# Attention in a two-layer kernel: four banks for the scores, probabilities turned back into the bank of their scores, two turnings in a row

## The reference, cut to what matters

```
NUM_HEADS = 16; NUM_GROUPS = 4; KEY_WIDTH = 64
Q = (X @ Wq).reshape(n, s, NUM_GROUPS, HEADS_PER_GROUP, KEY_WIDTH)
K = (X @ Wk).reshape(n, s, NUM_GROUPS, KEY_WIDTH)
V = (X @ Wv).reshape(n, s, NUM_GROUPS, VALUE_WIDTH)
raw = jnp.einsum('bsgwe,btge->bstgw', Q, K * scale)
attn = jax.nn.softmax(raw, axis=2)
A = jnp.einsum('bstgw,btge->bsgwe', attn, V).reshape(n, s, NUM_HEADS * VALUE_WIDTH)
P = A @ Wpost
return X + P
```

## Time and profile before

| what | us |
|---|---|
| median of 3 runs | 2735.33 |
| fastest and slowest of them | 2728.69, 2736.3 |
| the profiled execution | 2734.21 |
| its span, first to last instruction | 2732.1 |

### The profile page before, as it was taken

One profiled execution on the slowest core, in us unless ns is written; L12 is line 12 of the kernel. 1 busy time (PEld: TensorE's weight loads), 2 busy tenths in 40 slices (PEclk: granted clock), 3 DMA queues, 4 the chain that ended last, 5 costly groups with the idle time before them and its releaser, 6 DMA issues.

```text
span 2732.1 us, 38184 instructions
## 1 busy us (share of the span) xinstructions
PE 2280.7 (83%) x13155; PEld 1424.3 (52%) x13192; DVE 1884.1 (69%) x2830; ACT 1796.4 (66%) x3310; POOL 1738.2 (64%) x1416
## 2 busy tenths in 40 slices
PE   5776769999688889898989898989898988987781
PEld 4444547776445446554645465546544644554451
DVE  5779835553246786687668856876677667788788
ACT  3556834445367776788578857785787677765763
POOL 1000054434766998688878878877987797655565
PEclk9888989999899989899999999999999999998895
DMA  4000158874555667555755475447553854476786
GB/s 157 24 20 5 37 143 242 245 221 101 95 112 113 131 138 168 114 114 117 174 105 114 99 177 115 101 93 181 109 104 82 190 107 89 93 173 146 166 185 144
DMA packets 281904, 344.46 MB, mean 126 GB/s; under 512 B 66031, under 2 KB 211390, under 8 KB 281712
## 3 DMA queue, kind: packets, MB, share of 16 engines
q0 software_dynamic: 84080, 175.67, 34.4%
q1 hardware_dynamic: 175120, 144.80, 18.4%
q10 hardware_dynamic: 22512, 21.57, 2.3%
HBM read 198.23 MB, written 26.80 MB: 82 GB/s over the span
## 4 chain that ended last, share of the span: by engine, by line
PE 24%; POOL 18%; issue 12%; DVE 9%; ACT 9%; DMA 1%; POOLq 0%; another core or an unknown queue 0%; DVEq 0%; SPq 0%; ACTq 0%
POOL arena L1656 7%; POOL acc_sb L1634 5%; PE bank L1938 4%; PE bank L1907 4%; DVE bank L1531 3%; POOL arena L1662 3%; POOL arena L1672 3%; PE bank L1831 2%; PE bank L1774 2%; PE bank L1781 2%; PE bank L1793 2%; PE bank L1734 2%; ACT Pr L1040 2%; ACT bank L1157 1%; PE bank L1985 1%
## 5 line engine op out<-in xcount | busy, mean ns | idle before, releaser
L1656 POOL TENSOR_TENSOR arena<-arena 128x512 f32<-128x512 f32 x512 | 874.0, 1783 | 20.8 <-DVE arena L1522 11.1
L1634 POOL DMA_INDIRECT acc_sb<-ybuf,slot_idx x256 | 422.4, 1650 | 132.8 <-DMA ybuf<-arena 60.7
L1249 DVE TENSOR_REDUCE negmax<-bank 128x1 f32<-128x512 f32 x512 | 339.8, 680 | 232.4 <-PE bank L1774 230.9
L1157 ACT ACTIVATE bank<-arena,A_sb 128x512 f32<-128x512 f32 x512 | 353.3, 694 | 150.8 <-DVE arena L1536 132.2
L1040 ACT ACTIVATE Pr<-bank,negmax 128x512 f32<-128x512 f32 x512 | 358.5, 700 | 133.7 <-DVE negmax L1249 132.1
L1662 POOL TENSOR_TENSOR arena<-arena 128x512 f32<-128x512 f32 x192 | 297.5, 1550 | 230.9 <-DVE arena L1531 230.7
L1531 DVE TENSOR_TENSOR_SCAN bank<-bank,arena 128x512 f32<-128x512 f32 x320 | 390.0, 1219 | 68.8 <-ACT bank L1157 62.9
L1781 PE MATMUL bank<-ident,Pr 128*128 128x128 f32 x2048 | 344.0, 292 | 82.2 <-ACT PT L1022 78.9
L1781 PEld LDWEIGHTS bank<-ident,Pr 128*128 128x128 f32 x2048 | 230.9, 146 | 323.8 <-ACT PT L1022 175.8
L1022 ACT COPY PT<-bank 128x512 f32<-128x512 f32 x512 | 303.2, 592 | 135.2 <-PE bank L1781 99.2
L1774 PE MATMUL bank<-Kp,Qp 64*128 64x512 f32 x1024 | 305.4, 674 | 70.2 <-ACT Pr L1040 59.5
(11 more groups left out here) (214 smaller groups left out, 3842.1 us busy)
## 6 DMA issues: line engine op xcount, KB each, us to landing
arena<-arena POOLq DMA_DIRECT2D x255, 512.0 KB, 5.3
arena<-bc_dram SPq DMA_DIRECT2D x256, 256.0 KB, 3.9
ybuf<-arena ACTq DMA_DIRECT2D x64, 256.0 KB
arena<-in_w_gate SPq DMA_DIRECT2D x64, 128.0 KB
arena<-in_w_up SPq DMA_DIRECT2D x64, 128.0 KB
arena<-in_w_down SPq DMA_DIRECT2D x64, 128.0 KB
arena<-in_X SPq DMA_DIRECT2D x8, 512.0 KB, 8.4
s_sb<-in_X SPq DMA_DIRECT2D x8, 512.0 KB
```

The source lines that it names most:

```text
L1157: act.activation(bank[DECAY[g % 2]][:, :], dt_sb[:, size_slot(b, cb), :], ACT.Exp, scale=A_sb[:, cb, n:n + 1]).then_inc(ssm_decay, 1)
L1249: dve.tensor_reduce(negmax[:, m % RING_STAT:m % RING_STAT + 1], bank[m % RING_S_ATT][:, :], AX.X, ALU.max, negate=True).then_inc(att_max, 1)
L1634: pool.indirect_dma_start(acc_sb[:, i, :], None, ybuf, bass.IndirectOffsetOnAxis(ap=slot_idx[:, b * TILES + i, k:k + 1], axis=0), bounds_c ...
L1656: pool.tensor_tensor(st_sb[:, g % RING_S, :], u_sb[:, size_slot(b, cb), :], B_sb[:, load % RING_BC, :], ALU.mult).then_inc(ssm_input, 1)
```

## The change

Scores get four banks, 0 to 3, and bank `PROBT` is gone: T of tile m writes into bank m % 4, where its scores were. A bank is free only when C of its tile is done, so every wait of a later writer on `att_exp` (E) becomes one on `att_pt` (C). T comes one step earlier (lag 2 for 3), and in even steps the two S come before T on PE; so T of tile n-2 and T of tile n-1 follow each other, with the extra work P and V behind them. On ACT the order within a pair of steps becomes E, C, C, E, and the copy of P's result comes behind the second E instead of ahead of it. DVE's code for attention stays as it is. The core of the diff:

```
-RING_S_ATT, RING_P, RING_STAT = 3, 4, 4
+RING_S_ATT, RING_P, RING_STAT = 4, 4, 4
-LAG_EXP, LAG_T, LAG_AV, LAG_RAN = 1, 3, 4, 5
+LAG_EXP, LAG_T, LAG_AV, LAG_RAN = 1, 2, 4, 5
...
-    PROBT, AV, SIDE = 3, 4, 5
+    AV, SIDE = 4, 5
...
-            def att_step(self, b, n):
-                m = n - LAG_T
+            def copy_turned(self, b, m):
                 if 0 <= m < ATT_STEPS:
...
-                    act.copy(PT[:, m % RING_P, :, :].rearrange("p a b -> p (a b)"), bank[PROBT][:, :]).then_inc(att_pt, 1)
+                    act.copy(PT[:, m % RING_P, :, :].rearrange("p a b -> p (a b)"), bank[m % RING_S_ATT][:, :]).then_inc(att_pt, 1)
+
+            def att_step(self, b, n):
+
+                if n % 2 == 0:
+                    self.exponent(b, n - LAG_EXP)
+                    self.copy_turned(b, n - LAG_T)
+                    return
+                self.copy_turned(b, n - LAG_T)
+                self.exponent(b, n - LAG_EXP)
...
+            def spare_free(self, b, n):
+                w.wait_ge(att_pt, b * ATT_STEPS + min(n - RING_S_ATT + 2, ATT_STEPS))
+
             def product_k(self, b, g, n):
-                w.wait_ge(att_exp, b * ATT_STEPS + n - 1)
+                self.spare_free(b, n)
...
             def score(self, b, n):
 
-                if n + 1 >= RING_S_ATT:
-                    w.wait_ge(att_exp, b * ATT_STEPS + n + 1 - RING_S_ATT + 1)
+                if n >= RING_S_ATT:
+                    w.wait_ge(att_pt, b * ATT_STEPS + n + 1 - RING_S_ATT + 1)
...
             def turn_p(self, b, m):
                 w.wait_ge(att_exp, b * ATT_STEPS + m + 1)
-                w.wait_ge(att_pt, b * ATT_STEPS + m)
-                w.wait_ge(att_v, 2 * (b + 1))
                 for c in range(TILES):
-                    ins = pe.transpose(bank[PROBT][:, c * P:(c + 1) * P], Pr[:, m % RING_P, c * P:(c + 1) * P], ident[:, :])
+                    ins = pe.transpose(bank[m % RING_S_ATT][:, c * P:(c + 1) * P], Pr[:, m % RING_P, c * P:(c + 1) * P], ident[:, :])
...
                 p, at = n // PAIR_STEPS, n % PAIR_STEPS
+                if n % 2 == 0 and n < ATT_STEPS:
+                    self.score(b, n)
                 if 0 <= n - LAG_T < ATT_STEPS:
                     self.turn_p(b, n - LAG_T)
                 if n % 2 == 0:
-                    if n < ATT_STEPS:
-                        self.score(b, n)
                     return
```

More of the change, by code:

```diff
@@ L1031, in att_step, with exponent @@
                     self.copy_q(b, p + 1, spare(n))
-                m = n - LAG_EXP
+                if at == 1 and p >= 1:
+                    w.wait_ge(att_rec, PAIRS * b + p)
+                    w.wait_ge(att_invmm, PAIRS * b + p - 1)
+                    act.copy(rowinv[:, :, :], wide(rowrec[:, :], [[1, PAIR_STEPS], [0, HD]])).then_inc(att_inv, 1)
+            def exponent(self, b, m):
                 if 0 <= m < ATT_STEPS:
@@ L1041, in att_step @@
                                    accum_out=rowsum[:, p % 2, 2 * i + j:2 * i + j + 1]).then_inc(att_exp, 1)
[L1042 to L1046, removed]
             def exp_step(self, n):
@@ L1709, in att_begin @@
                 w.wait_ge(att_norm, 2 * (b + 1))
-                w.wait_ge(att_exp, ATT_STEPS * b)
+                w.wait_ge(att_pt, ATT_STEPS * b)
                 w.wait_ge(pool_const, 2)
@@ L1746, in att_lead @@
                 w.wait_ge(att_xT, 2 * (b + 1))
-                w.wait_ge(att_exp, b * ATT_STEPS)
                 if j == 0:
@@ L1765, in score @@
                     p, i, j = att_place(m)
[L1766 to L1770, removed]
+                    if 2 <= m < RING_S_ATT:
+                        w.wait_ge(att_v, 2 * b + m - 1)
                     w.wait_ge(att_q, PAIRS * b + p + 1)
@@ L1798, in spread @@
                 w.wait_ge(att_inv, PAIRS * b + p + 1)
-                w.wait_ge(att_exp, b * ATT_STEPS + min(n - 1, ATT_STEPS))
+                self.spare_free(b, n)
                 for i in range(TILES):
@@ L1826, in att_post @@
                 w.wait_ge(att_at, HEADS // 2 * (b + 1))
-                w.wait_ge(att_exp, ATT_STEPS * (b + 1))
+                w.wait_ge(att_pt, ATT_STEPS * (b + 1))
                 w.wait_ge(att_invbc, PAIRS * (b + 1))
@@ L1896, in tree_begin @@
                 w.wait_ge(x1_norm, 2 * (b + 1))
-                w.wait_ge(att_exp, ATT_STEPS * attended(b))
+                w.wait_ge(att_pt, ATT_STEPS * attended(b))
                 w.wait_ge(tree_act, 2 * TREES * b)
```

## The result

The changed kernel is slower: 2767.22 us median (2761.54 to 2770.35) against 2732.01 us, ratio 1.0139, 95% interval 1.0113 to 1.0165. The span of its profiled execution is 2764.3 us, 32.2 us longer than before. I had forecast 2700 us; the result lies at the upper end of the third rival, "C becomes the gate" (2743 to 2768 us), but, as will be seen, mostly not by that rival's mechanism.

What follows compares the result with a forecast made beforehand. No engine alone bounds the kernel; in the attention stretches four are 79% to 88% busy and PE waits. 122.4 us taken, 65 put back, 57 net, 35 reaching the end: 2735 - 35 = 2700 us, range 2660 to 2747.

Steps and rivals of the forecast that it cites:

- third rival: Beside the scan, P and S both wait for the newest C: 33 us more on PE, 2743 to 2768 us; chance 0.19.
- 57 us less waiting: PE's net gain in the six attentions beside the scan: 122.4 us of waits taken, 65 put back.
- Taken away: 122.4 us: PE's waits from 830 to 2420 us, at T for C and at S, products and spreadings for E, lose their reason.
- S waits for C of n-1 ... 35 us come back: On PE, S has V alone (1.02 us) as cover without P; half of the 70.3 us returns, 35 us.
- P waits for C ... 22 us: On PE, the extra work has only the second T (0.59 us) as cover; 0.2 us each, 108 times, 22 us.
- The E's moved copy costs nothing by itself as long as V (1.02 us) covers the copy: On ACT, the extra work's copy (about 0.6 us) goes behind E without cost of its own, covered by V.
- The wait of the second T for E ... 8 us: On PE, T of tile n-1 has 3.8 us of cover for its E in every pair; 8 us of waiting.
- T no longer waits for the previous C, since it has a bank of its own: On PE, 70.3 us of waits at T for the C ahead of it lose their reason.
- the rival on the clock: In the attention stretches the clock falls from 0.97 to 0.86, PE's work takes 114 us more, 2814 us; chance 0.02.
- The row with T busy 25.16 us at a clock of 1.00: Profile row cited to show more turning brings no lower clock: 1.00 with T alone busy 25.16 of 100 us.
- The sum had assumed that half or more of what PE gains gets through: Of 57 us, 0.8 passes in three stretches with attention's chain, 0.4 in three with POOL's: 23 and 12, together 35 us.

Runs made afterwards that it cites:

- Experiment 1: The changed kernel with ACT's copies of the extra work (K, Q, row sums) ahead of E again; 1.0034 of the kernel before.
- 13: The changed kernel with only K's and Q's copies ahead of E again, the row sums' still behind; 1.0118 of the kernel before.
- 17: The changed kernel with only the row sums' copies ahead of E again, K's and Q's still behind; 1.0071 of the kernel before.
- 2: The kernel before with all copies of the extra work moved behind E, nothing else; ratio 0.9995.
- 18: The kernel before with K's and Q's copies moved behind E, the row sums' left ahead of it; ratio 0.9965.
- Experiment 3: The kernel before with T and C one step earlier (lag 2 for 3), nothing else; ratio 1.0283.
- experiments 5 to 7: Maximum and E one step earlier: in the changed kernel 1.0717, in that with all copies ahead of E 1.0540, in the kernel before 1.0381.

## Why the prediction was wrong, by its own steps

Two steps failed, and a balance of PE's waits shows their sizes. I had forecast 57 us less waiting, and 28 us more came: 85 us between them. T's wait for E is 72.7 us of this (80.7 for 8) and S's wait for the copies 38.2 us (46.6 for 8.4), and the two terms for C, which were too large, take 25.7 us off (31.3 for 57). In time the distance is 2.7 points, from 2700 / 2735 = 0.987 to 1.0139. Experiment 1 gives 1.05 of them to the place of the copies. The other 1.6 are there with all copies ahead of E, where T waits 105.1 us for E; that this wait ate them is argued from the balance.

- "Taken away: 122.4 us" was right: none of these waits is left.
- "S waits for C of n-1 ... 35 us come back" and "P waits for C ... 22 us": the mechanism was right and both terms were too large, 19.6 and 11.7 us. The rival that I had built on them (C as the gate) is not what made it slower.
- "The E's moved copy costs nothing by itself as long as V (1.02 us) covers the copy" is the step that made the kernel slower than before, and it was put at nothing. I priced the extra work as the product's 1.81 us. The spreading is four transposes that take 0.56 us together, and it is 8 of the 18 in each batch. Behind it E doesn't fit, so S waited 27.9 us for `inv_bc`, with Q's 18.7 us beside it, and DVE waited 55.3 us for it at AT, a reader of the copy that my sum didn't have at all. Experiments 1, 13 and 17 put 1.05 of the 1.39 points on the copies and about two thirds of these or more on the row sums; experiments 2 and 18 show that in the old order the row sums' cost 0.3 points and K's and Q's gain 0.35.
- "The wait of the second T for E ... 8 us" is the step that cost the gain, wrong by ten times: 80.7 us. I counted cover in PE's own instructions, 3.8 us, and took it as the same that the extra work had. (The list that I gave for it, "T, T, V and two S", adds up to 3.26 us; with the S or the first T that also stands between it is 3.8.) But a step of the common order was gone between E and T, and in it stand the scan's and the head's pieces; in the timeline above ACT had three such operations ahead of the E while PE stood. Experiment 3 shows what such a step is worth in the old layout of banks and order (2.8%), and experiments 5 to 7 that it can't be had back from the step ahead of the maximum.
- "T no longer waits for the previous C, since it has a bank of its own" was true and of no use: the wait moved to E. Before, slack lay between E and T, and V hardly waited for C (0.9 us in all from 830 to 2450 us); the change moved a step from the first place to the second.
- The clock by stretch, 0.94 to 0.96 in the changed kernel against 0.94 to 0.97 before, went with PE busy 890.44 us for 890.20. So the rival on the clock, and the rule of the Trainium skill that the prediction cited beside it (TensorE: Matmul & The Clock Gate, Part 4: PE-mode transpose), do not explain the loss. The row with T busy 25.16 us at a clock of 1.00 is weaker than I made it: PE's other instructions ran in the same 100 us, in which it was busy 91.29 us in all.
- The sum had assumed that half or more of what PE gains gets through. As it went the other way, some 28 to 32 us more waiting on PE went with 32 us of time.
- The range, 2660 to 2747 us, was said to leave out the upper half of the third rival; it leaves out all of its 2743 to 2768 us but the first 4.

What stays open: with all copies ahead of E the changed order is still 0.34% slower (0.15 to 0.53). Its T waits 105.1 us for E, but shorter maxima and shorter exponents did not close the gap between the two orders (tried with the copies behind E only), and in bursts the 0.4% stayed. That the missing step between E and T is what remains is argued from experiment 3, not shown.

## What to carry to other kernels

Count a queue's cover in steps of the common order, foreign work included, not in one engine's own instructions; between the start and the end of a buffer's use the steps are fixed in number, and giving one to a wait takes it from another. Before an instruction is moved behind another because "the engine waits there anyway", look at the shortest of the cases in which it waits, and at every reader of its result: in the old order a copy behind an exponent paid behind a product of 1.81 us and cost behind a spreading of 0.56 us. Price the parts of a change apart, each in the old order too; a part that pays there (0.35%) was hidden in a change that cost 1.4%.

## What the runs showed that I had not expected

Moving only one engine's order has a steep price in in-order queues: the second T behind V on PE with ACT's C left in place gave 1.16, where 1.015 to 1.04 was expected (a part of it with a lower clock), and C ahead of E on ACT in even steps 1.076, which was near the top of what was expected, with no instruction added. And a quarter microsecond less per maximum (414 for 680 ns) or per exponent (485 for 700 ns), over 512 of each, gave 1.0 to 1.1% in the kernel before: some 28 to 30 us of the 110 to 136 us of busy time that was taken out.
